# First attention of a decoder stack: weight setup and the keys' maximum as one stage, maxima over 1024 columns at once

## The chip, the cores and the metric

The kernel runs on one core of a Trainium2 chip. The metric is the device time of one execution in microseconds, median of several. All engines of the core (TensorE, VectorE or DVE, ScalarE or ACT, GpSimd or POOL, SyncE or SP) run their own instruction streams and meet at semaphores. The kernel launches once and computes the whole decoder stack.

## The reference, cut to what matters

Two decoder layers over 128 sequences of 64 tokens (8192 tokens, 128 features). The change touches only the first block, an attention with random features:

```python
def _softmax_kernel_feats(data, proj, is_query):
    dn = 1.0 / jnp.sqrt(jnp.sqrt(jnp.float32(data.shape[-1])))
    ratio = 1.0 / jnp.sqrt(jnp.float32(proj.shape[0]))
    data_dash = jnp.einsum('bnhd,md->bnhm', data * dn, proj)
    diag = jnp.sum(jnp.square(data), axis=-1, keepdims=True) * (dn * dn) / 2.0
    if is_query:
        mx = jnp.max(data_dash, axis=-1, keepdims=True)
    else:
        mx = jnp.max(data_dash)
    return ratio * (jnp.exp(data_dash - diag - mx) + EPS_KERN)
...
k = jnp.einsum('bnd,dhk->bnhk', x, Wk)
kf = _softmax_kernel_feats(k, proj, False)
```

For the keys the maximum is taken over everything: all 8192 tokens, 16 heads and 64 features. So the kernel needs one pass over all tokens before the attention itself can begin.

## The kernel before, in words

`program` calls the stages one after the other; each is a `Phase` with its own semaphores, and at its end all engines meet at a barrier. The stages are the weights of the first attention (`setup_l0`), the keys' maximum (`phase_max`), the attention (`phase_performer`), its feed-forward block, and then the stages of the other four blocks, which the change doesn't touch.

**Setup** (`setup_l0`, lines 163 to 239). SP issues 17 loads on one queue (lines 190, 192): Wq, Wk, Wv, Wo, WqT and WkT of 512 KB each, W1 and W2 of 256 KB, eight small ones, and the projection matrix twice at the very end. TensorE and ACT wait for all of them. TensorE then joins projection and weights for queries and for keys (line 205, 16 float32 matmuls of 64 columns each), VectorE scales the results into `Wqp` and `Wkp` (line 214). The five matrices Wq, Wk, Wv, Wqp, Wkp (128x1024) are split into two float16 parts each: ACT writes the high part (line 236), VectorE the low part (line 219).

**Maximum** (`phase_max`, lines 272 to 357). The tokens are taken in 16 groups of 512 columns of the transposed x, two groups to a loop step (U = 2), the first step written out ahead of the loop by `peeled`. For each group SP loads 128x512 (line 301), ACT makes the high part (line 309), POOL the low part (line 317); both parts stay in SBUF (`xT_parts`) for the attention. TensorE then makes 8 tiles of 128x512 in 8 PSUM banks (`dd`), each out of three matmuls by the helper `thrice` (lines 158 to 160). VectorE takes the maximum of each tile (line 346) and folds the 8 columns into `acc` (line 349). TensorE may write a tile again when VectorE has read it (`part_ready`). Behind the loop the 128 maxima are brought to one and sent to all partitions (lines 332, 334, 352 to 356). Then the attention begins, with a barrier and two memsets of POOL (line 463) in front.

The pair of waits that ties TensorE and VectorE:

```python
pe.wait_ge(part_ready, TILES_HM * (U * it + j - 1) + i + 1)
thrice(nc, dd[i][:], [part[:, i, :] for part in Wkp], [part[:, group(it, j)] for part in xT_parts]).then_inc(dd_ready, 1)
...
dve.wait_ge(dd_ready, n)
nc.vector.tensor_reduce(part[j][:, i:i + 1], dd[i][:], AX, ALU.max).then_inc(part_ready, 1)
```

Of the kernel before, what the change touches and what calls it, by code (L numbers as in the profile page):

```python
# [10 lines left out]
ALU = mybir.AluOpType  # L11
# [151 lines left out]
def setup_l0(nc, ph, d, ident):  # L163

    DH, PAIRS = 64, H // 2
    DN = float(DH) ** -0.25
    PROJECTED = ("Wq", "Wk", "Wv", "Wqp", "Wkp")
# [6 lines left out]
    with Phase(nc, "s0") as t:  # L174
        wT = {k: t.sb(k, [P, PAIRS, D]) for k in ("WqT", "WkT")}
        whole = {k: t.sb(k, [P, PAIRS, P]) for k in PROJECTED}
        projT2 = t.sb("projT2", [P, DH])
        b2_rows, low_row = t.sb("b2_rows", [2, D]), t.sb("low_row", [2, 1])
        fused = [t.ps(f"fused{i}", [P, PAIRS, DH]) for i in range(4)]
        loaded, ones_ready, joined, scaled, high_ready, masked = (  # L180
            t.sem(n) for n in ("loaded", "ones_ready", "joined", "scaled", "high_ready", "masked"))
        loads = [(whole["Wq"], d["Wq"]), (whole["Wk"], d["Wk"]), (whole["Wv"], d["Wv"]), (w["Wo"], d["Wo"]), (wT["WqT"], d["WqT"]),
                 (wT["WkT"], d["WkT"]), (w["W1"], d["W1"]), (w["W2"], d["W2"]), (w["b1"], d["b1"]), (b2_rows, d["b2"].to_broadcast([2, D])), (low_row, d["low_row"]),
                 (w["ln1_g"], d["ln1_g"].to_broadcast([P, D])), (w["ln1_b"], d["ln1_b"].to_broadcast([P, D])),
                 (w["ln2_g"], d["ln2_g"].to_broadcast([P, D])), (w["ln2_b"], d["ln2_b"].to_broadcast([P, D]))]
        with nc.Block() as block:
            @block.sync
            def _(sp):
                for dst, src in loads:
                    sp.dma_start(dst[:], src[:]).then_inc(loaded, 16)  # L190
                for half in (slice(0, 64), slice(64, 128)):
                    sp.dma_start(projT2[half, :], d["projT"][:]).then_inc(loaded, 16)

            @block.gpsimd
            def _(pool):
                nc.gpsimd.memset(w["ones2"][:], 1.0).then_inc(ones_ready, 1)

            @block.tensor
            def _(pe):
                pe.wait_ge(loaded, 16 * (len(loads) + 2))  # L200
                for n, name in enumerate(("WqT", "WkT")):
                    for h in range(H):
                        half = slice(64 * (h % 2), 64 * (h % 2) + 64)

                        last = nc.tensor.matmul(fused[2 * n + h % 2][:, h // 2, :], wT[name][half, h // 2, :],
                                                projT2[half, :], start=True, stop=True)
                last.then_inc(joined, 1)

            @block.vector
            def _(dve):  # L210
                dve.wait_ge(joined, 1)
                for n, name in enumerate(("Wqp", "Wkp")):
                    for hh in range(2):
                        last = nc.vector.tensor_scalar(whole[name][:, :, 64 * hh:64 * hh + 64], fused[2 * n + hh][:], DN, None, ALU.mult)
                last.then_inc(scaled, 1)
                for n, k in enumerate(PROJECTED):

                    dve.wait_ge(high_ready, n + 1)
                    nc.vector.scalar_tensor_tensor(w[k][1][:].rearrange("p a b -> p (a b)"), whole[k][:].rearrange("p a b -> p (a b)"), L0_SCALE[k],
                                                   w[k][0][:].rearrange("p a b -> p (a b)"), ALU.mult, ALU.subtract)  # L220
                nc.vector.tensor_scalar(w["less_b1"][:], w["b1"][:], -1.0, None, ALU.mult)
                for n, (rows, parts) in enumerate(((b2_rows, w["b2_parts"]),)):

                    dve.wait_ge(high_ready, len(PROJECTED) + n + 1)
                    nc.vector.tensor_scalar(parts[:], parts[:], low_row[:], None, ALU.mult).then_inc(masked, 1)
                    dve.wait_ge(masked, n + 1)
                    nc.vector.tensor_tensor(parts[:], rows[:], parts[:], ALU.subtract)
                dve.wait_ge(ones_ready, 1)

            @block.scalar  # L230
            def _(act):
                act.wait_ge(loaded, 16 * (len(loads) + 2))
                for n, k in enumerate(PROJECTED):
                    if n == 3:
                        act.wait_ge(scaled, 1)
                    nc.scalar.activation(w[k][0][:], whole[k][:], ACT.Copy, scale=L0_SCALE[k]).then_inc(high_ready, 1)
                for rows, parts in ((b2_rows, w["b2_parts"]),):
                    nc.scalar.activation(parts[:], rows[:], ACT.Copy).then_inc(high_ready, 1)
    return w
# [32 lines left out]
def phase_max(nc, xT, Wkp, shared_mx, xT_parts):  # L272


    GROUP, U, TILES_HM = 512, 2, 8
    steps = TOK // (GROUP * U)
    with Phase(nc, "mx") as ph:
        x_sb = [ph.sb(f"x{j}", [P, GROUP]) for j in range(U)]
        dd = [ph.ps(f"dd{i}", [P, 512]) for i in range(TILES_HM)]
        part = [ph.sb(f"part{j}", [P, TILES_HM]) for j in range(U)]  # L280
        acc = ph.sb("acc", [P, TILES_HM])
# [4 lines left out]
        dd_ready, part_ready, acc_ready, small, moved, high_ready, low_ready = (  # L286
            ph.sem(n) for n in ("dd_ready", "part_ready", "acc_ready", "small", "moved", "high_ready", "low_ready"))
        ident = shared_mx["ident"]
# [3 lines left out]

        with nc.Block() as block:
            @block.sync
            def _(sp):
                def body(it):
                    for j in range(U):
                        if not is_first(it):

                            sp.wait_ge(low_ready, U * it + (j + 1 - U))  # L300
                        sp.dma_start(x_sb[j][:], xT[:, bass.ds((U * it + j) * GROUP, GROUP)]).then_inc(loaded[j], 16)
                peeled(nc.sync, steps, body)

            @block.scalar
            def _(act):
                def body(it):
                    for j in range(U):
                        act.wait_ge(loaded[j], 16 * (it + 1))
                        nc.scalar.activation(xT_parts[0][:, group(it, j)], x_sb[j][:], ACT.Copy).then_inc(high_ready, 1)
                peeled(nc.scalar, steps, body)  # L310

            @block.gpsimd
            def _(pool):
                def body(it):
                    for j in range(U):
                        pool.wait_ge(high_ready, U * it + j + 1)
                        nc.gpsimd.tensor_tensor(xT_parts[1][:, group(it, j)], x_sb[j][:], xT_parts[0][:, group(it, j)], ALU.subtract).then_inc(low_ready, 1)
                peeled(nc.gpsimd, steps, body)

            @block.tensor  # L320
            def _(pe):
                def body(it):
                    for j in range(U):
                        pe.wait_ge(low_ready, U * it + j + 1)
                        for i in range(TILES_HM):
                            if not (is_first(it) and j == 0):

                                pe.wait_ge(part_ready, TILES_HM * (U * it + j - 1) + i + 1)
                            thrice(nc, dd[i][:], [part[:, i, :] for part in Wkp], [part[:, group(it, j)] for part in xT_parts]).then_inc(dd_ready, 1)
                peeled(nc.tensor, steps, body)  # L330
# [6 lines left out]
            def _(dve):  # L337
                nc.vector.memset(acc[:], -3.0e38).then_inc(acc_ready, 1)
                nc.vector.memset(ones_row[:], 1.0)

                def body(it):
                    for j in range(U):
                        for i in range(TILES_HM):
                            n = TILES_HM * (U * it + j) + i + 1
                            dve.wait_ge(dd_ready, n)
                            nc.vector.tensor_reduce(part[j][:, i:i + 1], dd[i][:], AX, ALU.max).then_inc(part_ready, 1)
# [2571 lines left out]
```

## Time and profile before

| what | value |
|---|---|
| median of 3 runs | 4009.61 us (4009.27, 4009.61, 4018.98) |
| the profiled execution, its own time | 4014.4 us |
| its span, first to last instruction | 4012.6 us |
| TensorE busy | 3414.4 us, 85% |
| VectorE busy | 3038.1 us, 76% |
| ScalarE busy | 2356.9 us, 59% |
| GpSimd busy | 1842.3 us, 46% |
| mean granted TensorE clock | 0.915 |

Times in the trace are microseconds from the span's start. A line such as L346 is a line of the kernel; where a helper issues the instruction (lines 158 to 160) the tile's name tells whose it is. `s_` tiles belong to the setup, `mx_` tiles to the maximum, `b_` tiles to the attention. "SPq" is SP's issue of a DMA, "PEld" a weight load of TensorE, and in brackets stands how long an engine sat idle before a row and what ended that.

### The profile page before, as it was taken

The numbers are of one execution on the slowest core, as the hardware profiler recorded it, in microseconds if no ns is written. First come the engines' busy times: TensorE is split into PE (matmuls) and PEld (weight loads), VectorE is DVE, ScalarE is ACT, GpSimd is POOL, SyncE is SP. The second block draws the span as 40 slices with busy tenths as digits, with TensorE's granted clock in tenths as the row PEclk, the third lists the DMA queues.
The fourth block names the chain that finished last, engine by engine and source line by source line (L and its number), as shares of the span: only waits on it lengthen the run. The fifth ranks groups of instructions, "written<-read, shape, count | busy, mean of one in ns | idle before, by whom it ended". The sixth has DMA issues, their size and how long they took to land. (4 is left out here: it accounts for less than half of the span.)

```text
span 4012.6 us, 91730 instructions
## 1 busy us (share of the span) xinstructions
PE 3414.4 (85%) x30917; PEld 2194.5 (55%) x30917; DVE 3038.1 (76%) x6227; ACT 2356.9 (59%) x5257; POOL 1842.3 (46%) x2322
## 2 busy tenths in 40 slices
PE   6899999998665882899999968888399999999998
PEld 3466666665444872566666657777244444444443
DVE  6777777776674662899999948888588888888887
ACT  1355555654763442799899946565355555555555
POOL 1000000000553663677777722222187777778776
PEclk9999999999887775899999978898699999999999
DMA  2000000000112212000000012222376565556663
GB/s 82 6 11 9 10 9 10 10 9 25 43 51 64 67 49 41 17 18 20 18 18 18 12 46 57 55 58 54 110 160 139 128 136 126 131 126 138 132 136 85
DMA packets 279473, 243.93 MB, mean 61 GB/s; under 512 B 57832, under 2 KB 205324, under 8 KB 279308
## 3 DMA queue, kind: packets, MB, share of 16 engines
q1 hardware_dynamic: 267916, 237.21, 24.9%
q10 hardware_dynamic: 11392, 4.79, 0.5%
q8 instruction: 70, 1.15, 0.1%
q14 instruction: 95, 0.78, 0.1%
HBM read 210.34 MB, written 31.59 MB: 60 GB/s over the span
## 5 line engine op out<-in xcount | busy, mean ns | idle before, releaser
L2650 POOL TENSOR_TENSOR d_hidden<-d_gated,d_upper 128x512 f32<-128x512 f32 x528 | 802.2, 1544 | 259.8 <-DVE d_upper L2759 131.7
L2766 DVE TENSOR_TENSOR d_h_low<-d_hidden,d_h_high 128x512 f16<-128x512 f32 x528 | 540.8, 1024 | 118.1 <-ACT d_h_high L2726 116.8
L2720 ACT ACTIVATE d_gated<-d_g 128x512 f32<-128x512 f32 x528 | 315.2, 597 | 493.2 <-PE d_u L2666 493.2
L750 POOL MEMSET f_minus_half<- 128x4 f32 x1 | 0.1, 101 | 864.4 <-POOLq L37 864.4
L2759 DVE TENSOR_TENSOR d_upper<-d_u,d_coef 128x512 f32<-128x512 f32 x512 | 349.2, 682 | 61.4 <-issue 28.2
L2726 ACT ACTIVATE d_h_high<-d_hidden 128x512 f16<-128x512 f32 x528 | 328.4, 622 | 8.2 <-POOL d_hidden L2650 8.2
L1825 ACT ACTIVATE c_sc<-c_sc,c_negmax 128x129 f32<-128x129 f32 x1024 | 326.3, 394 | 9.0 <-issue 4.0
L2664 PE MATMUL d_g<-d_x_high,w_Wg_high 128*128 128x512 f16 x528 | 201.8, 382 | 92.4 <-DVE d_upper L2759 56.1
L1653 POOL TENSOR_TENSOR c_posg<-w_pos,c_gate 128x512 f32<-128x512 f32 x256 | 265.9, 1039 | 0.0
L1732 PE MATMUL c_turned<-all_ident,c_sc 128*128 128x128 f32 x1024 | 180.6, 302 | 35.4 <-ACT c_sc L1825 34.6
L2664 PE MATMUL d_o<-d_h_high,w_Wd_high 128*128 128x512 f16 x528 | 201.4, 381 | 2.0 <-ACT d_h_high L2726 1.6
L2664 PE MATMUL d_u<-d_x_high,w_Wu_high 128*128 128x512 f16 x528 | 202.0, 383 | 0.0
L2665 PE MATMUL d_u<-d_x_high,w_Wu_low 128*128 128x512 f16 x528 | 201.9, 382 | 0.0
L2665 PE MATMUL d_g<-d_x_high,w_Wg_low 128*128 128x512 f16 x528 | 201.8, 382 | 0.0
L2666 PE MATMUL d_u<-d_x_low,w_Wu_high 128*128 128x512 f16 x528 | 201.7, 382 | 0.0
L2666 PE MATMUL d_g<-d_x_low,w_Wg_high 128*128 128x512 f16 x528 | 201.6, 382 | 0.0
L2666 PE MATMUL d_o<-d_h_low,w_Wd_high 128*128 128x512 f16 x528 | 201.4, 381 | 0.0
L2665 PE MATMUL d_o<-d_h_high,w_Wd_low 128*128 128x512 f16 x528 | 201.4, 381 | 0.0
L1937 DVE TENSOR_REDUCE c_negmax<-c_sc 128x4 f32<-128x516 f32 x256 | 176.9, 691 | 8.8
L1935 DVE SCALAR_TENSOR_TENSOR c_sc<-c_scores,c_posg 128x512 f32<-128x512 f32 x256 | 173.4, 678 | 5.3 <-POOL c_posg L1653 2.9
L561 ACT ACTIVATE b_sq<-b_a 128x1024 f32<-128x1024 f32 x64 | 65.6, 1025 | 181.2 <-PE b_a L160 181.2
L1830 ACT ACTIVATE c_pT<-c_turned 128x512 f32<-128x512 f32 x256 | 150.0, 586 | 36.3 <-PE c_turned L1732 36.0
(408 smaller groups left out, 9649.8 us busy)
## 6 DMA issues: line engine op xcount, KB each, us to landing
d_coef<-coefT SPq DMA_DIRECT2D x256, 512.0 KB, 7.2
d_cT<-in_ctxT SPq DMA_DIRECT2D x128, 64.0 KB, 2.0
mx_x<-in_xT SPq DMA_DIRECT2D x16, 256.0 KB
b_x<-in_x SPq DMA_DIRECT2D x64, 64.0 KB
y<-b_y SPq DMA_DIRECT2D x64, 64.0 KB, 1.6
f_y<-y SPq DMA_DIRECT2D x16, 256.0 KB, 3.9
f_x<-in_x SPq DMA_DIRECT2D x16, 256.0 KB, 3.7
x<-f_res SPq DMA_DIRECT2D x16, 256.0 KB, 2.4
```

The source lines that it names most:

```text
L1653: nc.gpsimd.tensor_tensor(posg[a][:], w["pos"][:, hs, :], gate[s][:, hs].unsqueeze(2).to_broadcast([T, 4, T]), ALU.mult).then_inc(posg_rea ...
L1732: last = nc.tensor.transpose(tbank[a % 2][:, i, :], sc[slot(j)][:, 4 * a + i, 0:T], w["ident"][:])
L1825: last = nc.scalar.activation(sc[s][:, h, :], sc[s][:, h, :], ACT.Exp, bias=negmax[s][:, h:h + 1], scale=-1.0)
L1937: nc.vector.tensor_reduce(negmax[s][:, hs], sc[s][:, hs, :], AX, ALU.min).then_inc(top_ready, 1)
L2650: nc.gpsimd.tensor_tensor(hidden[b][:], gated[b][:], upper[b][:], ALU.mult).then_inc(h_ready, 1)
L2664: nc.tensor.matmul(out, weights[0], high, start=start, stop=False)
L2665: nc.tensor.matmul(out, weights[1], high, start=False, stop=False)
L2666: return nc.tensor.matmul(out, weights[0], low, start=False, stop=stop)
L2720: nc.scalar.activation(gated[b][:], ps_g[i][:], ACT.Silu, scale=1.0 / W_SCALE).then_inc(silu_ready, 1)
L2726: nc.scalar.activation(h_high[b][:], hidden[b][:], ACT.Copy).then_inc(h_high_ready, 1)
L2759: nc.vector.tensor_tensor(upper[b][:], ps_u[i][:], coef[c % CBUFS][:, u % CU, :], ALU.mult).then_inc(upper_ready, 1)
L2766: nc.vector.tensor_tensor(h_low[b][:], hidden[b][:], h_high[b][:], ALU.subtract).then_inc(h_low_ready, 1)
```

## The change

`setup_l0` becomes `weights_l0`, which only allocates, and `whole_l0`, which allocates the whole matrices; all work of the setup goes into `phase_max`, so one stage with one barrier stands where there were two.

- SP loads WkT, the projection matrix (twice), group 0 of the tokens, WqT and group 1 first, each with semaphores of their own, and then the other 13 in one row; the loop's token loads come behind them.
- TensorE joins the key weights, then the query weights, into the PSUM tiles `dd[2]` and `dd[3]`, then starts with the products.
- Of the key matrix VectorE scales one half and ACT the other; ACT writes the high part, VectorE the low part. The split of the other four matrices is made behind the last tokens, by ACT (now two instructions for each, a scaling in place and a copy) and POOL (the subtraction, on VectorE before).
- `dd` is 4 tiles of 128x1024 (two banks each) in place of 8 of 128x512. The matmuls are the same 24 for a group; VectorE takes 4 maxima over 1024 columns in place of 8 over 512, and the waits are for a pair of banks.
- The bias rows (three small VectorE instructions) come ahead of the last loop step's maxima.

The diff, cut to its core:

```diff
-        dd = [ph.ps(f"dd{i}", [P, 512]) for i in range(TILES_HM)]
+        dd = [ph.ps(f"dd{i}", [P, 2 * GROUP]) for i in range(WIDE)]
+        fused = dict(Wkp=dd[2], Wqp=dd[3])
...
+                sp.dma_start(whole["WkT"][:], d["WkT"][:]).then_inc(keys_loaded, 16)
+                for half in (slice(0, 64), slice(64, 128)):
+                    sp.dma_start(whole["projT2"][half, :], d["projT"][:]).then_inc(keys_loaded, 16)
+                load_x(0, 0)
+                sp.dma_start(whole["WqT"][:], d["WqT"][:]).then_inc(queries_loaded, 16)
+                load_x(0, 1)
+                for dst, src in rest:
+                    sp.dma_start(dst[:], src[:]).then_inc(rest_loaded, 16)
+                with nc.sync.Fori(1, steps) as it:
                     for j in range(U):
...
+                        sp.wait_ge(low_ready, U * it + (j + 1 - U))
+                        load_x(it, j)
...
+                for j in range(U):
+                    high(0, j)
+                act.wait_ge(joined, 1)
+                out, of = halves("Wkp", 1)
+                nc.scalar.activation(out, of, ACT.Copy, scale=DN).then_inc(other_scaled, 1)
+                act.wait_ge(other_scaled, 1)
+                act.wait_ge(half_scaled, 1)
+                nc.scalar.activation(w["Wkp"][0][:], whole["Wkp"][:], ACT.Copy, scale=L0_SCALE["Wkp"]).then_inc(key_high, 1)
+                act.wait_ge(joined, 2)
+                for hh in range(2):
+                    out, of = halves("Wqp", hh)
+                    nc.scalar.activation(out, of, ACT.Copy, scale=DN).then_inc(query_scaled, 1)
...
+                act.wait_ge(rest_loaded, 16 * len(rest))
+                nc.scalar.activation(w["b2_parts"][:], whole["b2_rows"][:], ACT.Copy).then_inc(row_high, 1)
+                act.wait_ge(query_scaled, 2)
+                for n, k in enumerate(SPLIT):
+                    nc.scalar.activation(whole[k][:], whole[k][:], ACT.Copy, scale=L0_SCALE[k]).then_inc(scaled, 1)
+                    act.wait_ge(scaled, n + 1)
+                    nc.scalar.activation(w[k][0][:], whole[k][:], ACT.Copy).then_inc(split_high, 1)
...
+                for n, k in enumerate(SPLIT):
+                    pool.wait_ge(split_high, n + 1)
+                    nc.gpsimd.tensor_tensor(flat(w[k][1]), flat(whole[k]), flat(w[k][0]), ALU.subtract).then_inc(split_low, 1)
...
+                    for i in range(WIDE):
+                        if not (is_first(it) and j == 0):
+                            pe.wait_ge(part_ready, WIDE * (U * it + j - 1) + i + 1)
+                        elif i == 3:
+                            pe.wait_ge(query_scaled, 2)
+                        for a in range(2):
+                            last = thrice(nc, dd[i][:, GROUP * a:GROUP * (a + 1)], [p[:, 2 * i + a, :] for p in w["Wkp"]], [p[:, group(it, j)] for p in xT_parts])
+                        last.then_inc(dd_ready, 1)
...
+                pe.wait_ge(keys_loaded, 16 * 3)
+                join("WkT", "Wkp")
+                pe.wait_ge(queries_loaded, 16)
+                join("WqT", "Wqp")
+                pe.wait_ge(key_low, 1)
...
+                    for i in range(WIDE):
+                        dve.wait_ge(dd_ready, WIDE * (U * it + j) + i + 1)
+                        nc.vector.tensor_reduce(part[j][:, i:i + 1], dd[i][:], AX, ALU.max).then_inc(part_ready, 1)
```

How the instructions stand. On SP, from the program's start, before:

```order
L190 DMA s_Wq<-in_attn_Wq 128x1024
L190 DMA s_Wk<-in_attn_Wk 128x1024
L190 DMA s_Wv<-in_attn_Wv 128x1024
L190 DMA w_Wo<-in_attn_Wo 128x1024
L190 DMA s_WqT<-in_attn_WqT 128x1024
L190 DMA s_WkT<-in_attn_WkT 128x1024
L190 DMA w_W<-in_attn_W 128x512 x2
```

and with the change:

```order
L263 DMA s_WkT<-in_attn_WkT 128x1024
L265 DMA s_projT<-in_attn_projT 64x64 x2
L261 DMA mx_x<-in_xT 128x512
L267 DMA s_WqT<-in_attn_WqT 128x1024
L261 DMA mx_x<-in_xT 128x512
L270 DMA s_Wq<-in_attn_Wq 128x1024
L270 DMA s_Wk<-in_attn_Wk 128x1024
L270 DMA s_Wv<-in_attn_Wv 128x1024
L270 DMA w_Wo<-in_attn_Wo 128x1024
L270 DMA w_W<-in_attn_W 128x512 x2
```

The key weights moved from place 6 to the front and the projection matrix from the last place to the second; the tokens stood in another stage.

On VectorE, at the same place, before (`s_fused` are the joined weights in PSUM, `mx_part` the maxima of one group):

```order
L214 TENSOR_SCALAR s_Wqp<-s_fused 128x8x64 x2
L214 TENSOR_SCALAR s_Wkp<-s_fused 128x8x64 x2
L219 SCALAR_TENSOR_TENSOR w_Wq_low<-s_Wq,w_Wq_high 128x1024
L219 SCALAR_TENSOR_TENSOR w_Wk_low<-s_Wk,w_Wk_high 128x1024
L219 SCALAR_TENSOR_TENSOR w_Wv_low<-s_Wv,w_Wv_high 128x1024
L219 SCALAR_TENSOR_TENSOR w_Wqp_low<-s_Wqp,w_Wqp_high 128x1024
L219 SCALAR_TENSOR_TENSOR w_Wkp_low<-s_Wkp,w_Wkp_high 128x1024
```

and with the change:

```order
L371 TENSOR_SCALAR s_Wkp<-mx_dd 128x8x64 [waits mx_joined]
L373 SCALAR_TENSOR_TENSOR w_Wkp_low<-s_Wkp,w_Wkp_high 128x1024 [waits mx_key_high]
L362 TENSOR_REDUCE mx_part<-mx_dd 128x1 [waits mx_dd_ready] x4
L365 TENSOR_TENSOR mx_acc<-mx_acc,mx_part 128x4 [waits mx_acc_ready,mx_part_ready]
L362 TENSOR_REDUCE mx_part<-mx_dd 128x1 [waits mx_dd_ready] x4
```

Only one scaling and one subtraction are left ahead of the first maximum; the four other subtractions left this engine. They stand on POOL now, behind its loop over the tokens:

```order
L309 TENSOR_TENSOR parts_xT_low<-mx_x,parts_xT_high 128x512
L314 REGISTER_ALU
L314 COMPARE_AND_BRANCH
L319 TENSOR_TENSOR w_Wq_low<-s_Wq,w_Wq_high 128x1024 [waits mx_split_high]
L319 TENSOR_TENSOR w_Wk_low<-s_Wk,w_Wk_high 128x1024 [waits mx_split_high]
L319 TENSOR_TENSOR w_Wv_low<-s_Wv,w_Wv_high 128x1024 [waits mx_split_high]
L319 TENSOR_TENSOR w_Wqp_low<-s_Wqp,w_Wqp_high 128x1024 [waits mx_split_high]
```

## Rows read from the trace of the kernel before

**Rows 1.** The page, busy time of each engine
```profile
PE 3414.4 (85%) x30917; PEld 2194.5 (55%) x30917; DVE 3038.1 (76%) x6227; ACT 2356.9 (59%) x5257; POOL 1842.3 (46%) x2322
```

**Rows 2.** Timeline, 0 to 60 us: start, duration, engine, line, instruction, count, idle before
```profile
1.98 0.40 SPq L190 DMA_DIRECT2D s_Wq<-in_attn_Wq  x1
...
9.30 1.22 SPq L192 DMA_DIRECT2D s_projT<-in_attn_projT  x2
...
18.40 3.68 PE L205 MATMUL s_fused<-s_projT,s_WqT 64*128 64x64 f32 x32 [18.40 <-DMA s_projT<-in_attn_projT]
...
21.86 3.62 PE L205 MATMUL s_fused<-s_projT,s_WkT 64*128 64x64 f32 x32
25.54 1.29 DVE L214 TENSOR_SCALAR s_Wqp<-s_fused 128x512 f32<-128x512 f32 x2 [25.54 <-PE s_fused L205]
...
29.02 1.04 ACT L236 ACTIVATE w_Wkp_high<-s_Wkp 128x1024 f16<-128x1024 f32 x1
...
32.48 1.22 DVE L219 SCALAR_TENSOR_TENSOR w_Wkp_low<-s_Wkp,w_Wkp_high 128x1024 f16<-128x1024 f32 x1
...
34.94 25.16 SPq L301 DMA_DIRECT2D mx_x<-in_xT  x11
...
37.75 1.26 ACT L309 ACTIVATE parts_xT_high<-mx_x 128x512 f16<-128x512 f32 x2 [7.50 <-DMA mx_x<-in_xT]
38.47 2.26 POOL L317 TENSOR_TENSOR parts_xT_low<-mx_x,parts_xT_high 128x512 f16<-128x512 f32 x2 [36.30 <-ACT parts_xT_high L309]
...
39.68 0.61 PE L158 MATMUL mx_dd<-parts_xT_high,w_Wkp_high 128*128 128x512 f16 x1 [14.19 <-POOL parts_xT_low L317]
```

**Rows 3.** Windows: stretch, its length, busy per engine, granted clock, DMA share, GB/s
```profile
3.00:4.00 1.00, 0.00 (x0) 0.00 (x0) 0.00 (x0) 0.26 (x1) 0.00 (x0) 1.00 0.91 254
...
11.00:12.00 1.00, 0.00 (x0) 0.00 (x0) 0.00 (x0) 0.00 (x0) 0.00 (x0) 1.00 1.01 401
...
16.00:17.00 1.00, 0.00 (x0) 0.00 (x0) 0.00 (x0) 0.00 (x0) 0.00 (x0) 1.00 0.33 36
```

**Rows 4.** Groups, 34 to 130 us: shapes, count, busy us, mean ns, idle before
```profile
L346 DVE TENSOR_REDUCE mx_part<-mx_dd 128x1 f32<-128x512 f32 x128 | 78.5, 680 | 9.8 <-PE mx_dd L160 9.0 <-issue 0.7
L158 PE MATMUL mx_dd<-parts_xT_high,w_Wkp_high 128*128 (+1 forms) x128 | 49.7, 388 | 14.2 <-POOL parts_xT_low L317 14.2
```

**Rows 5.** Timeline, TensorE: clock step at 45 us, last product at 125 us
```profile
45.13 0.38 PE L159 MATMUL mx_dd<-parts_xT_low,w_Wkp_high 128*128 128x512 f16 x1
...
124.99 0.38 PE L160 MATMUL mx_dd<-parts_xT_high,w_Wkp_low 128*128 x1
```

**Rows 6.** Timeline, VectorE: one loop step of two groups, and the end
```profile
97.20 4.87 DVE L346 TENSOR_REDUCE mx_part<-mx_dd 128x1 f32<-128x512 f32 x8 [0.32 <-PE mx_dd L160]
...
107.60 4.87 DVE L346 TENSOR_REDUCE mx_part<-mx_dd 128x1 f32<-128x512 f32 x8 [0.32 <-PE mx_dd L160]
...
123.00 4.87 DVE L346 TENSOR_REDUCE mx_part<-mx_dd 128x1 f32<-128x512 f32 x8
...
128.11 0.16 DVE L352 TENSOR_REDUCE mx_col<-mx_acc 128x1 f32<-128x8 f32 x1
...
129.38 0.16 DVE L356 COPY w_key_max<-mx_dd 128x1 f32<-128x1 f32 x1 [0.47 <-PE mx_dd L334]
```

**Rows 7.** Timeline, GpSimd and VectorE at 48 us
```profile
48.42 1.15 POOL L317 TENSOR_TENSOR parts_xT_low<-mx_x,parts_xT_high 128x512 f32 x1 [2.41 <-ACT parts_xT_high L309]
48.43 1.16 DVE L349 TENSOR_TENSOR mx_acc<-mx_acc,mx_part 128x8 f32<-128x8 f32 x1
```

**Rows 8.** Timeline, VectorE in the attention stage: a 1024-column reduction, then the next
```profile
148.27 1.22 DVE L624 TENSOR_REDUCE b_top<-b_b 128x16 f32<-128x1024 f32 x1 [1.56 <-PE b_b L160]
149.41 0.68 DVE L609 TENSOR_SCALAR b_kf<-b_kf 128x1024 f32<-128x1024 f32 x1
```

**Rows 9.** Windows of a later stage, all f32 on TensorE: columns as in rows 3
```profile
2356.00:2358.00 2.00, 2.00 (x19) 1.96 (x17) 1.52 (x4) 1.01 (x2) 0.00 (x0) 0.50 0.00 0
2358.00:2360.00 2.00, 2.00 (x11) 2.00 (x11) 0.04 (x1) 0.33 (x2) 0.00 (x0) 0.50 0.00 0
```

More of the change, by code:

```diff
@@ L173, in setup_l0 @@
              ln2_g=ph.sb("ln2_g", [P, D]), ln2_b=ph.sb("ln2_b", [P, D]))
[L174 to L238, printed above, removed]
@@ L239, in setup_l0, with whole_l0 @@
-    return w
+    return w
+def whole_l0(t):
+    DH, PAIRS = 64, H // 2
+    whole = {k: t.sb(k, [P, PAIRS, P]) for k in PROJECTED}
+    whole.update({k: t.sb(k, [P, PAIRS, D]) for k in ("WqT", "WkT")})
+    whole.update(projT2=t.sb("projT2", [P, DH]), b2_rows=t.sb("b2_rows", [2, D]), low_row=t.sb("low_row", [2, 1]))
+    return whole
 def setup_cross0(nc, ph, d, ident):
@@ L269, in setup_cross0, with phase_max @@
     return w
[L272 to L275 removed]
+def phase_max(nc, w, whole, d, xT, xT_parts):
+    GROUP, U, PAIRS, WIDE = 512, 2, H // 2, 4
+    DN = 64.0 ** -0.25
+    SPLIT = ("Wq", "Wk", "Wv", "Wqp")
     steps = TOK // (GROUP * U)
@@ L278, in phase_max @@
         x_sb = [ph.sb(f"x{j}", [P, GROUP]) for j in range(U)]
-        dd = [ph.ps(f"dd{i}", [P, 512]) for i in range(TILES_HM)]
-        part = [ph.sb(f"part{j}", [P, TILES_HM]) for j in range(U)]
-        acc = ph.sb("acc", [P, TILES_HM])
+        dd = [ph.ps(f"dd{i}", [P, 2 * GROUP]) for i in range(WIDE)]
+        fused = dict(Wkp=dd[2], Wqp=dd[3])
+        part = [ph.sb(f"part{j}", [P, WIDE]) for j in range(U)]
+        acc = ph.sb("acc", [P, WIDE])
         col = ph.sb("col", [P, 1])
@@ L304, in _, with high @@
             @block.scalar
             def _(act):
-                def body(it):
-                    for j in range(U):
-                        act.wait_ge(loaded[j], 16 * (it + 1))
-                        nc.scalar.activation(xT_parts[0][:, group(it, j)], x_sb[j][:], ACT.Copy).then_inc(high_ready, 1)
-                peeled(nc.scalar, steps, body)
+                def high(it, j):
+                    act.wait_ge(loaded[j], 16 * (it + 1))
+                    nc.scalar.activation(xT_parts[0][:, group(it, j)], x_sb[j][:], ACT.Copy).then_inc(high_ready, 1)
@@ new lines, in _ @@
+                for hh in range(2):
+                    out, of = halves("Wqp", hh)
+                    nc.scalar.activation(out, of, ACT.Copy, scale=DN).then_inc(query_scaled, 1)
+                with nc.scalar.Fori(1, steps) as it:
+                    for j in range(U):
+                        high(it, j)
+                act.wait_ge(rest_loaded, 16 * len(rest))
+                nc.scalar.activation(w["b2_parts"][:], whole["b2_rows"][:], ACT.Copy).then_inc(row_high, 1)
+                act.wait_ge(query_scaled, 2)
@@ L318, in _, with low @@
-                peeled(nc.gpsimd, steps, body)
+                def low(it, j):
+                    pool.wait_ge(high_ready, U * it + j + 1)
+                    nc.gpsimd.tensor_tensor(xT_parts[1][:, group(it, j)], x_sb[j][:], xT_parts[0][:, group(it, j)], ALU.subtract).then_inc(low_ready, 1)
+                nc.gpsimd.memset(w["ones2"][:], 1.0).then_inc(ones_ready, 1)
+                for j in range(U):
+                    low(0, j)
+                with nc.gpsimd.Fori(1, steps) as it:
+                    for j in range(U):
+                        low(it, j)
@@ L320, in _ @@
+                for n, k in enumerate(SPLIT):
+                    pool.wait_ge(split_high, n + 1)
+                    nc.gpsimd.tensor_tensor(flat(w[k][1]), flat(whole[k]), flat(w[k][0]), ALU.subtract).then_inc(split_low, 1)
+                pool.wait_ge(split_low, len(SPLIT))
+                pool.wait_ge(ones_ready, 1)
             @block.tensor
             def _(pe):
-                def body(it):
-                    for j in range(U):
[L324 to L329, printed above, removed]
@@ L330, in _, with join, products @@
-                peeled(nc.tensor, steps, body)
+                def join(source, name):
+                    for h in range(H):
+                        half = slice(64 * (h % 2), 64 * (h % 2) + 64)
+                        last = nc.tensor.matmul(halves(name, h % 2)[1][:, h // 2, :], whole[source][half, h // 2, :], whole["projT2"][half, :], start=True, stop=True)
+                    last.then_inc(joined, 1)
+                def products(it, j):
+                    pe.wait_ge(low_ready, U * it + j + 1)
+                    for i in range(WIDE):
[6 more added lines that the diff above has]
+                        last.then_inc(dd_ready, 1)
@@ L331, in _ @@
+                pe.wait_ge(keys_loaded, 16 * 3)
[3 more added lines that the diff above has]
+                pe.wait_ge(key_low, 1)
+                for j in range(U):
+                    products(0, j)
+                with nc.tensor.Fori(1, steps) as it:
+                    for j in range(U):
+                        products(it, j)
                 pe.wait_ge(small, 1)
@@ L338, in _ @@
                 nc.vector.memset(acc[:], -3.0e38).then_inc(acc_ready, 1)
                 nc.vector.memset(ones_row[:], 1.0)
-                def body(it):
-                    for j in range(U):
[L343 to L346, printed above, removed]
-                        dve.wait_ge(part_ready, TILES_HM * (U * it + j + 1))
-                        dve.wait_ge(acc_ready, U * it + j + 1)
-                        nc.vector.tensor_tensor(acc[:], acc[:], part[j][:], ALU.max).then_inc(acc_ready, 1)
@@ L350, in _ @@
-                peeled(nc.vector, steps, body)
+                dve.wait_ge(joined, 1)
+                out, of = halves("Wkp", 0)
+                nc.vector.tensor_scalar(out, of, DN, None, ALU.mult).then_inc(half_scaled, 1)
+                dve.wait_ge(key_high, 1)
+                nc.vector.scalar_tensor_tensor(flat(w["Wkp"][1]), flat(whole["Wkp"]), L0_SCALE["Wkp"], flat(w["Wkp"][0]), ALU.mult, ALU.subtract).then_inc(key_low, 1)
+                for j in range(U):
+                    tops(0, j)
@@ new lines, in _ @@
+                with nc.vector.Fori(1, steps - 1) as it:
+                    for j in range(U):
+                        tops(it, j)
+                dve.wait_ge(row_high, 1)
+                nc.vector.tensor_scalar(w["less_b1"][:], w["b1"][:], -1.0, None, ALU.mult)
+                nc.vector.tensor_scalar(w["b2_parts"][:], w["b2_parts"][:], whole["low_row"][:], None, ALU.mult).then_inc(row_masked, 1)
+                dve.wait_ge(row_masked, 1)
+                nc.vector.tensor_tensor(w["b2_parts"][:], whole["b2_rows"][:], w["b2_parts"][:], ALU.subtract)
@@ L351, in _ @@
+                for j in range(U):
+                    tops(steps - 1, j)
                 dve.wait_ge(acc_ready, U * steps + 1)
```

44 lines of the change are left out of this document (26 added, 18 removed).

## The prediction

> **What bounds the kernel now.** I read the page first: TensorE is busy 85% of the span [rows 1], but the change touches only its first 130 us, and those must be read by themselves. The timeline from 0 shows three pieces in a row. First nothing computes until all 17 loads have landed: TensorE's first matmul starts at 18.40, released by the projection matrix, the last load issued [rows 2]. Then comes a chain of small steps: joins 18.40 to 25.54, scaling, five splits (the last ends at 32.48 + 1.22 = 33.70), a barrier, the first token load issued at 34.94, its high part at 37.75, its low part, and the first product at 39.68 [rows 2]. From there the products run: the groups list 128 matmuls on each of three lines, 384 in all, and only one idle stretch of TensorE, the 14.2 us ahead of the first [rows 4]. The first 12 start every 0.43 us or so; from 45.13 to 124.99 the other steps are (124.99 - 45.13) / 370 = 0.216 us each [rows 5]. That is 512 columns at 1.2 GHz and then at 2.4 GHz. So TensorE bounds this piece, but VectorE nearly does: one loop step (two groups) takes it 107.60 - 97.20 = 10.40 us with 0.32 idle, against 48 x 0.216 = 10.36 us on TensorE [rows 5, 6], and at the end it is late: the last product ends at 124.99 + 0.38 = 125.37, the final maximum starts at 128.11 [rows 5, 6]. The way from there to the key maximum, 1.4 us, and on to the attention, is the same in both kernels.
>
> **The front.** New start of the products, step by step. SP begins at 1.98 and spends 0.40 on a large issue and 1.22 on the two projection issues [rows 2], so the last load that the key join needs is issued by 3.6. Before, two 256 KB token loads issued from 34.94 were in use at 37.75, 2.8 us later [rows 2]; WkT is as many bytes, and the queue moves 401 GB/s when full [rows 3]. From the second projection issue (3.0) that gives 5.8; I take 5.7, with 5.1 to 6.7 as bounds. The two joins take 25.54 - 18.40 = 7.14 us for both matrices [rows 2], 3.6 each, so keys are joined at 9.3 and queries at 12.8. Between these the key chain runs on VectorE and ACT: half a scaling 0.68 (1.29 for two) on each engine side by side, the high part 1.04, the low part 1.22 [rows 2], about 2.9 with nothing else, so ready at 12.2, under the query join. ACT has first to make the high parts of groups 0 and 1, 0.63 each; group 1 is the fifth load, issued at about 4.7, so in use at 7.5 to 8 and done by 9, just ahead of the key chain. POOL's two low parts (2.26) are done by 10.5. Nothing is later than the query join: **products start at 12.84 in place of 39.68, -26.84 us**. The whole second wait, for tokens, and one barrier are gone in this number.
>
> **The products.** The same 384 matmuls in the same order: 0. Whether the slow 0.43 us steps come again is open: the engine now comes from 7 us of float32 joins instead of 14.2 us of idleness. What rows show is that float32 work need not raise the clock: in a later stage TensorE is busy 2.00 of 2.00 us twice in a row on small float32 matmuls and the granted clock stays 0.50 [rows 9]. So I take 0, bounds 0 and -2.6 (12 x 0.216), and the products end at 12.84 + 85.69 = 98.53. The Trainium skill ("TensorE: Matmul & The Clock Gate", Part 1) says that the slow clock is the default and that sustained matmul activity releases it; by that the joins would do the warming, and the sum would be 2.6 us lower. It comes back as a rival.
>
> **The maxima.** Before, a reduction of 512 costs 4.87 / 8 = 0.61 us in a row [rows 6]. A 1024-column one from two PSUM banks stands in the attention: 1.22 alone, and the next instruction starts 1.14 later [rows 8]. So 8 x 1.14 = 9.1 for a loop step in place of 16 x 0.61 = 9.8, and VectorE's step falls from 10.40 to about 9.75, under TensorE's 10.36. No gain while TensorE bounds, but at the end VectorE is no longer late: it has one 1024 reduction left (1.22) and the fold (0.24 from 127.87 to 128.11), 1.5 us in place of 128.11 - 125.37 = 2.74: **-1.25 us**.
>
> **What moved under cover.** SP's 13 other loads now stand ahead of the loop's token loads. The 17 issues took 8.5 us before [rows 2]; with two token issues the loop's first comes at about 11.5. The bytes (4.0 MB before, 4.5 now) drained by 17 to 18 us before, the end of it slowly, 36 GB/s in small pieces [rows 3]; 0.5 MB more is 1.3 us, and group 2 behind it 0.7. It lands at about 20, and its parts take 0.63 + 1.15: ready at 22. Group 2 is due when groups 0 and 1 are through, 12.84 + 2.6 + 48 x 0.216 = 25.8. Cover of some 4 us; 0. Each later pair comes every 5 us as before, twice as fast as it is used, so the tokens end near 55 us. Behind them ACT's 8 passes of 1.04 and POOL's 4 subtractions, 2.3 each (twice 1.13), end near 66, with 32 us of products left to hide them: 0. The three bias instructions cost VectorE 0.7 us once, inside its new slack.
>
> The moved subtractions can still hurt. At 48.43 VectorE's fold, else 0.17 or so, took 1.16, exactly as long as POOL's subtraction at 48.42 [rows 7]. The Trainium skill ("GPSIMD Engine Reference", 8. Key points) states the cause, a shared SBUF interface and contention when VectorE has two SBUF inputs; rows 7 agree. POOL's new instructions are 2.3 us, so two folds may each wait up to 2.3. TensorE may run three wide tiles ahead, 3.9 us, before it stands. I take 0, bounds 0 and +2.
>
> **Sum.** -26.84 - 1.25 = -28.1 us. Against the profiled execution: 4014.4 - 28.1 = 3986.3. That execution is 4.8 above the median of 4009.6, so against the median **3981.5 us**, 0.7% faster. A measurement of this kernel can tell about 0.3% (12 us) from no change.
>
> **Rivals.**
> - *Warm start* (0.22). The joins lift the clock, all 384 products run at 0.216, the first ones too. For: nothing stands between joins and products now. Against: rows 9. 3978.9.
> - *Backlog or starved supply* (0.14). VectorE falls behind through POOL's long subtractions, or group 2 lands after 25.8, and TensorE stands a few us, perhaps falling back to 1.2 GHz once, which costs 2.6. For: rows 7, and the slow drain in rows 3. Against: 4 us of cover in both. +3 to +6, about 3986.
> - *The order of loads does nothing* (0.07). The loads share the engines, so the first ones land with the last at 18.4. For: all were waited for together before, so no row shows one landing early. The joins would end at 25.54, the key chain is covered, and the products start there: saving 39.68 - 25.54 + 1.25 = 15.4. 3994.2.
> - *Wide maxima bound the stage, slower than before* (0.03). If a reduction across two banks that TensorE is filling in turn is slowed, VectorE bounds. There are 64; VectorE's slack is 0.08 each, and 28.1 / 64 = 0.44, so it decides from 1.14 + 0.52 = 1.66 us each; at 1.8 the stage gains 64 x 0.58 = 37 and the kernel takes 4018. Against: rows 8, where two banks cost the same per column as one.
> - The rest (0.04): the later stages move by themselves, or the start is otherwise late and the result within 0.3%.
>
> **How the numbers follow.** The forecast has 0.50 and gives 3981.5. The range takes in the warm start and the early end of the key load below (3978.9 less 0.6, less 2 for a median that may fall lower), and above the backlog and what the runs of one kernel differ by (three within 10 us, the profiled one 4.8 up): 3976 to 3991. Late loads and slower are left out. Faster by over 0.3% (under 3997.6): 0.94; within 0.3%: 0.03; slower: 0.03.
>
> **What the profile would show.** Right: first join at 5 to 7 us, first product near 12.8 with almost no idle ahead of it, key maximum copied near 101.4 in place of 129.38, wide maxima 1.22 us each with VectorE waiting for TensorE at most of them, one idle stretch of TensorE only. The step from 0.43 to 0.216 some 5 us behind the first product, or none (warm start). Wrong: a first join past 10 us; TensorE idle ahead of the third group; folds of 2 us with TensorE idle behind them; wide maxima over 1.3 us.

## The result and the profile after

The changed kernel takes 3958.76 us (median of 5, 3957.47 to 3965.34) against 4009.27 us for the kernel before (5 runs, 4000.43 to 4018.98): ratio 0.9878, 95% interval 0.9862 to 0.9894. The interval lies wholly below 1: the kernel got faster by 1.2%, and by nearly twice what was forecast: 50.5 us, not 28.1. The profiled execution took 3959.03 us, 55.4 less than the profiled one of before (4014.4, which is itself some 5 above the median); stage by stage I compare these two.

The page of the changed kernel, its span, busy times and one DMA queue; the first two answer to [rows 1]:

```profile
span 3957.2 us, 91525 instructions
...
PE 3417.1 (86%) x30917; PEld 2203.3 (56%) x30917; DVE 3024.6 (76%) x6156; ACT 2363.6 (60%) x5264; POOL 1850.8 (47%) x2326
...
q14 instruction: 68, 0.56, 0.0%
```

The engines are nearly as busy as before (VectorE 13.5 us less, GpSimd 8.5 more, of over 3950). So hardly any work has gone; idle time has. Queue 14, which loads instructions, moved 95 packets before and moves 68 now. I come back to that line.

**The first stage.** The timeline of the first 20 us, which answers to [rows 2]:

```profile
1.97 0.40 SPq L263 DMA_DIRECT2D s_WkT<-in_attn_WkT  x1
...
2.43 1.20 SPq L265 DMA_DIRECT2D s_projT<-in_attn_projT  x2
...
4.78 0.43 SPq L261 DMA_DIRECT2D mx_x<-in_xT  x1
...
6.16 3.67 PE L328 MATMUL mx_dd<-s_projT,s_WkT 64*128 64x64 f32 x32 [6.16 <-DMA s_projT<-in_attn_projT]
...
9.68 3.68 PE L328 MATMUL mx_dd<-s_projT,s_WqT 64*128 64x64 f32 x32
...
9.89 0.69 DVE L371 TENSOR_SCALAR s_Wkp<-mx_dd 128x512 f32<-128x512 f32 x1 [7.63 <-PE mx_dd L328]
...
10.27 0.63 ACT L280 ACTIVATE parts_xT_high<-mx_x 128x512 f16<-128x512 f32 x1 [1.23 <-DMA mx_x<-in_xT]
...
10.81 0.58 ACT L286 ACTIVATE s_Wkp<-mx_dd 128x512 f32<-128x512 f32 x1
...
11.42 1.06 ACT L289 ACTIVATE w_Wkp_high<-s_Wkp 128x1024 f16<-128x1024 f32 x1
...
12.51 1.22 DVE L373 SCALAR_TENSOR_TENSOR w_Wkp_low<-s_Wkp,w_Wkp_high 128x1024 f16<-128x1024 f32 x1 [1.93 <-ACT w_Wkp_high L289]
...
13.79 0.61 PE L158 MATMUL mx_dd<-parts_xT_high,w_Wkp_high 128*128 128x512 f16 x1 [0.43 <-DVE w_Wkp_low L373]
...
16.75 0.61 PE L159 MATMUL mx_dd<-parts_xT_low,w_Wkp_high 128*128 128x512 f16 x1
...
17.17 0.40 PE L160 MATMUL mx_dd<-parts_xT_high,w_Wkp_low 128*128 128x512 f16 x1
```

The last product, TensorE's timeline (answers to [rows 5]):

```profile
98.14 0.38 PE L160 MATMUL mx_dd<-parts_xT_high,w_Wkp_low 128*128 x1
```

VectorE's timeline with two maxima groups of one step, and the end (answers to [rows 6]):

```profile
79.49 4.74 DVE L362 TENSOR_REDUCE mx_part<-mx_dd 128x1 f32<-128x1024 f32 x4 [0.24 <-issue]
84.27 0.16 DVE L365 TENSOR_TENSOR mx_acc<-mx_acc,mx_part 128x4 f32<-128x4 f32 x1
84.37 5.05 DVE L362 TENSOR_REDUCE mx_part<-mx_dd 128x1 f32<-128x1024 f32 x4
...
100.00 0.16 DVE L387 TENSOR_REDUCE mx_col<-mx_acc 128x1 f32<-128x4 f32 x1
...
101.27 0.16 DVE L391 COPY w_key_max<-mx_dd 128x1 f32<-128x1 f32 x1 [0.47 <-PE mx_dd L355]
```

The key maximum is copied at 101.27 in place of 129.38: 28.11 us earlier, the very sum forecast, in part by luck, as the last part tells. The slow steps end at 17.17 after eight matmuls, where twelve were slow before, and the last product ends at 98.14 + 0.38 = 98.52.

**The rest.** Of the 55.4 us between the two profiled executions 27.3 are still without a cause. I looked for the stage in which they lie by the first and last start of one line in each stage. At the attention's first maximum the distance is 28.0 us (135.3 to 107.3), at the start of the last stage, the mixture of experts, 25.6; so between them nothing was won, 2.4 were lost. Then the last stage itself, ACT's gate of which there are 528 (duration min, median and max in ns, then first and last start), before:

```profile
L2720 ACT ACTIVATE d_gated<-d_g x528: 597/597/599, 2896.7 to 3997.3; 128x512 f32<-128x512 f32 x176
```

and with the change:

```profile
L2755 ACT ACTIVATE d_gated<-d_g x528: 597/597/599, 2871.1 to 3941.8; 128x512 f32<-128x512 f32 x176
```

3997.3 - 2896.7 = 1100.6 us before, 3941.8 - 2871.1 = 1070.7 now: **29.9 us in a stage whose code the change doesn't touch**. With the 25.6 ahead of it that makes 55.5, the whole difference. The waits inside its loop (in total, times, longest), before:

```profile
PE d_g L2664 <- DVE d_upper L2759: 43.2, 25, 4.3
...
DVE d_upper L2759 <- issue: 28.2, 5, 5.9
```

after:

```profile
PE d_g L2699 <- DVE d_upper L2794: 23.5, 20, 1.4
...
DVE d_upper L2794 <- PE d_u L2701: 3.6, 10, 0.4
```

Five times VectorE sat idle, for 5.6 us in the mean, before its first instruction of a loop step, and nothing in the profile released it ("issue"). Five is the number of times that this loop jumps back: the stage has eight steps, the first and the last are written out, and the loop between them runs six rounds. With the change the five are gone. One of them in VectorE's timeline, before:

```profile
3162.22 0.68 DVE L2766 TENSOR_TENSOR d_h_low<-d_hidden,d_h_high 128x512 f16<-128x512 f32 x1
3168.80 0.69 DVE L2759 TENSOR_TENSOR d_upper<-d_u,d_coef 128x512 f32<-128x512 f32 x1 [5.91 <-issue]
```

and the windows around it (PE, PEld, DVE, ACT, POOL busy, granted clock, DMA share, GB/s):

```profile
3160.00:3164.00 4.00, 4.00 (x20) 1.85 (x19) 2.86 (x3) 2.24 (x5) 2.72 (x2) 1.00 0.67 200
3164.00:3168.00 4.00, 1.33 (x7) 0.39 (x4) 0.00 (x0) 1.11 (x2) 0.03 (x1) 1.00 0.46 122
3168.00:3172.00 4.00, 2.36 (x6) 0.87 (x7) 2.96 (x4) 0.00 (x0) 2.28 (x2) 0.53 0.01 2
```

VectorE ends a step at 3162.90 and begins the next at 3168.80. TensorE runs dry behind it (busy 1.33 of 4 us), and the granted clock falls to half for some of the time that follows. What VectorE waited for shows in the DMA view, in the line of queue 14. From 3160 to 3170, around this one stretch, before:

```profile
q14 instruction: 3, 0.02, 0.8%
```

Over the loop, before (3140 to 3870):

```profile
q14 instruction: 26, 0.21, 0.1%
```

and after (3100 to 3840):

```profile
q14 instruction: 3, 0.02, 0.0%
```

26 packets of instructions (8 KB each, 0.21 MB by 26) against 3, and these 3 come when the loop is through: from 3100 to 3810 queue 14 has no packet at all with the change. So before, code was loaded again at every jump back of the loop. That it is VectorE's code is an inference up to here; e1 and e2 below test it.

### The profile page after: what moved, and what is told of

The parts are those of the page before. It is cut to its first block and busy times, and to the rows that moved or that the text cites. A ratio compares the mean times of both kernels' runs of the same rounds, so it can differ in the third digit from the quotient of the medians.

```text
span 3957.2 us, 91525 instructions
## 1 busy us (share of the span) xinstructions
PE 3417.1 (86%) x30917; PEld 2203.3 (56%) x30917; DVE 3024.6 (76%) x6156; ACT 2363.6 (60%) x5264; POOL 1850.8 (47%) x2326
## 5 line engine op out<-in xcount | busy, mean ns | idle before, releaser
L2198 POOL TENSOR_TENSOR d_kB<-d_kT,w_variant 128x512 f32<-128x512 f32 x64 | 73.2, 1144 | 211.7 <-ACT d_kT L2352 211.7
```

## The experiments

**Is it the place of VectorE's instructions?** The change took 23 instructions out of VectorE's stream ahead of the last loop (2325 stand there in place of 2348; counted in the program, without branches and without the waits that are instructions of their own). TensorE lost 10, ACT gained 5. With branches and waits 3043 instructions stand there in place of 3068, which is 25 fewer, so the 23 below bring the loop back to within two instructions of its old place. To tell the engines apart I gave only VectorE its 23 back, as memsets while it is idle:

```diff
+        filler = ph.sb("filler", [P, 128])
...
                 nc.vector.memset(ones_row[:], 1.0)
+                for n in range(23):
+                    nc.vector.memset(filler[:, n:n + 1], 0.0)
```

> The changed kernel with 23 tiny memsets more on VectorE at its start, where it sits idle from 2.3 to 9.9 us, so that its last loop stands at the same place of VectorE's instruction stream as before (2348 instructions ahead of it; 2325 with the change). Theory 1, the 27 us beyond the first stage come from code loading on VectorE in the last stage's loop: the five idle stretches of some 5.6 us that end in 'issue' come back there, the last stage takes 1100 us again in place of 1070, total 3980 to 3990. Theory 2, TensorE's code or its clock history does it: nothing changes, 3959. Theory 3, it is only scatter between executions: no steady difference, within 4 us of the changed kernel. The first stage ends at 101.3 in all three.

Measured: 3989.08 us (4 runs, 3986.17 to 3991.16), ratio to before 0.9935 (0.9918 to 0.9951); key maximum at 102.29. VectorE's group in the last stage:

```profile
L2797 DVE TENSOR_TENSOR d_upper<-d_u,d_coef 128x512 f32<-128x512 f32 x512 | 349.1, 682 | 64.1 <-issue 30.7 <-PE d_u L2704 11.2 <-DMA d_coef<-coefT 10.8
```

The five "issue" stretches are back, 30.7 us, and queue 14 shows 94 packets. The 23 memsets take 0.58 us together at the program's start and cost 30 us more than 3.1 ms later. TensorE's stream was the changed one; its code is not the cause, nor is scatter. (The key maximum came 1.0 us later than expected: the products began at 14.17, and eleven of them were slow.)

The other way round, the kernel before with 105 memsets ahead of `dve.wait_ge(joined, 1)`:

> The kernel before with 105 tiny memsets on VectorE ahead of its first wait, hidden behind the loads; 105 = 128 - 23, so if code is loaded in blocks of 128 instructions (8 KB at 64 bytes) the last loop stands in its block as in the changed kernel. Theory 1 with that block: the five stretches go, total about 4009 - 25 = 3984, with the first stage ending at 129.4 as before. Theory 1 with another block size: no change. Theories 2 and 3: no change, 4009.

Measured: 3989.64 us (3978.51 to 3995.48) against 4014.70, ratio 0.9929 (0.9908 to 0.9949); the first stage still ends at 127.92. VectorE's group:

```profile
L2762 DVE TENSOR_TENSOR d_upper<-d_u,d_coef 128x512 f32<-128x512 f32 x512 | 349.1, 682 | 30.5 <-DMA d_coef<-coefT 11.1 <-PE d_u L2669 6.5 <-issue 0.4
```

0.4 us of "issue" in place of 28.2, 70 packets on queue 14. So the kernel before could have had these 25 us by itself (by the interval, 20 to 37; this kernel's four runs lie 17 us apart). A control with 41 memsets in the same spot:

> A control for e2: the kernel before with 41 memsets in place of 105, so that 2389 instructions stand ahead of VectorE's last loop, a place that had the five stretches in e6. By the border theory nothing changes against before, ratio 1.000, and the stretches are there. If the memsets in the kernel before gain by themselves (by timing, not by place), it is faster, 4000 or less.

Measured: 4011.29 us against 4014.98, ratio 0.9989 (0.9975 to 1.0003), "issue" 30.9 us, 94 packets. Memsets alone do nothing; the place does.

**Where are the good places?** Three more in the changed kernel:

> The changed kernel with 12 tiny memsets more on VectorE at its start: 2337 instructions ahead of its last loop, between the changed kernel (2325, no stretch) and e1 (2348, five stretches of some 6 us). If a border of a code block decides, it is one or the other and nothing between: last stage 1070 or 1100 us, total 3959 or 3988. If the stretch grew with each instruction it would be about half, 3974.

Measured: 3954.69 us, ratio to before 0.9855 (0.9833 to 0.9877), no stretch.

> The same with 64 memsets more (2389 instructions ahead of the last loop), 41 behind e1, 41 ahead of the place that is the changed kernel's again if code comes in blocks of 128. Theory with a border: either clean, 3959, or five stretches, 3988; it tells on which side the clean places lie. A theory in which the number of instructions matters, not the place, has stretches at 23 and so also at 64.

Measured: 3988.43 us, 0.9934 (0.9909 to 0.9960), five stretches of 5.2 to 5.4 us.

> The changed kernel with 90 memsets more (2415 ahead of the last loop), between e6 (2389, stretches) and the place of e2 (2453, none). Either clean, 3959, or five stretches, 3988; it narrows down the share of places that are clean, which is the chance that an unrelated edit to VectorE's stream costs or gains some 28 us.

Measured: 3962.70 us, 0.9856 (0.9827 to 0.9885), no stretch, 69 packets on queue 14. (The page of e6 has 95 there, that of e5 68.)

| instructions ahead of VectorE's last loop | kernels | last stage, us | "issue" stretches |
|---|---|---|---|
| 2325, 2326 (e4) | after, e7, e4 | 1070.7 (after), 1070.9 (e7), 1069.3 (e4) | none |
| 2329 | e8 | 1069.4 | none |
| 2337 | e5 | 1069.0 | none |
| 2348 | before, e1 | 1100.6, 1101.6 | five |
| 2357 | e3 | 1098.7 | five |
| 2389 | e6, e9 | 1095.8, 1095.9 | five |
| 2415 | e10 | 1069.1 | none |
| 2453 | e2 | 1071.0 | none |

All or nothing, with borders between 2337 and 2348 and between 2389 and 2415, and the place of 2325 good again 128 further on. A sum that grows with the number of instructions is out. With branches and waits counted, the kernels made from the one before (before, e2, e9) stand two instructions further than the table says, so e2 is 130 and not 128 behind the changed kernel; the order of the rows stays, and both borders with it.

**The terms of the first stage.** Narrow maxima in the new stage (eight PSUM tiles of 512 columns, `WIDE = 8`, one `thrice` to a tile):

```diff
-                        for a in range(2):
-                            last = thrice(nc, dd[i][:, GROUP * a:GROUP * (a + 1)], [p[:, 2 * i + a, :] for p in w["Wkp"]], [p[:, group(it, j)] for p in xT_parts])
+                        last = thrice(nc, dd[i][:], [p[:, i, :] for p in w["Wkp"]], [p[:, group(it, j)] for p in xT_parts])
```

> The changed kernel with 8 PSUM tiles of 512 columns and 8 maxima a group, as before; all else kept. By my sum the key maximum comes 1.25 us later (101.27 to 102.5), since VectorE is late at the end again; a rival says that the wide maxima also keep TensorE from standing still, and then the products themselves end later than 98.5. VectorE has 32 instructions more ahead of its last loop than with the change, 9 more than before; by theory 1 the last stage may lose its 28 us again for that alone, total 3960 to 3990.

Measured: 3994.29 us, 0.9956 (0.9940 to 0.9973), with the stretches; 4 us above the range expected. The key maximum comes 0.96 us later, not 1.25, though the products began 0.6 earlier. The stage's end, VectorE and TensorE:

```profile
100.66 0.16 DVE L386 TENSOR_REDUCE mx_col<-mx_acc 128x1 f32<-128x8 f32 x1
...
102.23 0.16 DVE L390 COPY w_key_max<-mx_dd 128x1 f32<-128x1 f32 x1 [0.67 <-PE mx_dd L354]
```

```profile
96.97 0.38 PE L160 MATMUL mx_dd<-parts_xT_high,w_Wkp_low 128*128 x1
100.87 0.37 PE L352 MATMUL mx_dd<-all_ident,mx_col 128*1 128x128 f32 x1 [3.52 <-DVE mx_col L386]
```

TensorE's last product ends 96.97 + 0.38 = 97.35 (the products started at 13.19 and only some five of them were slow), and VectorE takes until 100.66 to begin the final maximum, 3.3 us late; in the changed kernel it is 1.5. TensorE has no wait for VectorE in the loop either way, so within this stage the wide maxima bring what stands behind the last product, 1.8 us here, and nothing else.

The load order of before in the new stage (Wq, Wk, Wv, Wo, WqT, WkT and the rest, the projection last, then groups 0 and 1):

> The changed kernel with the loads issued in the order of before (keys sixth, projection last, then two token groups), still one stage. My sum of the front: the joins start at 18.4, end at 25.5, the tokens are there at about 20, so the products start at 25.8 and the key maximum comes 12 us later than in the changed kernel, 113.3; total 3971. VectorE's instructions stand where they do with the change, so no stretch in the last loop. If the front's gain came from dropping the barrier and the second wait alone, the key maximum stays near 101 to 105.

Measured: 3971.48 us, 0.9899 (0.9877 to 0.9921); key maximum at 113.57. TensorE's timeline:

```profile
19.06 3.68 PE L330 MATMUL mx_dd<-s_projT,s_WkT 64*128 64x64 f32 x32 [19.06 <-DMA s_projT<-in_attn_projT]
...
26.08 0.61 PE L158 MATMUL mx_dd<-parts_xT_high,w_Wkp_high 128*128 128x512 f16 x1
```

The order of the loads is worth 12.3 us (113.57 - 101.27); what is left of the 28.1, some 16, came from making one stage out of two, and the tail (1.3).

The four late subtractions on VectorE, ahead of the last loop step's maxima:

```diff
+                for n, k in enumerate(SPLIT):
+                    dve.wait_ge(split_high, n + 1)
+                    nc.vector.tensor_tensor(flat(w[k][1]), flat(whole[k]), flat(w[k][0]), ALU.subtract).then_inc(split_low, 1)
```

> The changed kernel with the four late subtractions on VectorE instead of GpSimd, ahead of the last loop step's maxima, where VectorE has little slack. By my sum of the cover: 4 x 1.2 = 4.9 us more on VectorE, TensorE may run 3.9 us ahead, so it stands about 1 us or more, and the key maximum comes 2 to 5 us later, 103 to 106; total 3961 to 3964. A rival says that GpSimd's long subtractions cost VectorE as much where they are now: then nothing changes.

Measured: 3966.29 us, 0.9878 (0.9848 to 0.9907), too scattered (3952.95 to 3971.05) for a verdict by the total; the stage itself is clear, key maximum at 106.07, 4.8 us late. The first of VectorE's subtractions, the wait of TensorE, and a window just behind it (columns as in [rows 3]):

```profile
90.56 1.21 DVE L383 TENSOR_TENSOR w_Wq_low<-s_Wq,w_Wq_high 128x1024 f16<-128x1024 f32 x1
```

```profile
PE mx_dd L158 <- DVE mx_part L359: 2.7, 1, 2.7
```

```profile
96.00:98.00 2.00, 1.55 (x4) 0.65 (x5) 2.00 (x3) 0.00 (x0) 0.00 (x0) 0.53 0.00 0
```

TensorE stood 2.7 us, and when it went on the granted clock was 0.53 from 96 to 98. So the pause was paid for twice: of the 4.8 us, 0.3 are a later start of the products (14.12), 2.7 the pause, and the remaining 1.8, by my estimate, the slow matmuls behind it. On GpSimd the same four cost the stage nothing.

**The clock.** Nine float16 matmuls on a tile of ones ahead of the key join:

```diff
+                pe.wait_ge(warm_ready, 1)
+                for _ in range(9):
+                    nc.tensor.matmul(dd[0][:, 0:512], warm[:, 0:128], warm[:], start=True, stop=True)
                 pe.wait_ge(keys_loaded, 16 * 3)
```

> The changed kernel with nine float16 matmuls of 512 columns on a tile of ones ahead of the key join, while the loads are under way. If the clock rises before the joins and float32 joins hold it, the products start at 0.216 us a step: the 8 slow steps go, key maximum 1.7 us earlier, at 99.6. If the joins let it fall, the products start slowly again and nothing is gained. If the joins themselves run faster at the higher clock, they take less than 3.5 us each.

Measured: 3961.05 us, 0.9873 (0.9855 to 0.9892), not to be told from the changed kernel. TensorE:

```profile
2.69 3.90 PE L345 MATMUL mx_dd<-mx_warm 128*128 128x512 f16 x9 [2.69 <-DVE mx_warm L371]
6.52 2.00 PE L329 MATMUL mx_dd<-s_projT,s_WkT 64*128 64x64 f32 x32
9.21 3.23 PE L329 MATMUL mx_dd<-s_projT,s_WqT 64*128 64x64 f32 x32 [0.69 <-DMA s_WqT<-in_attn_WqT]
13.32 0.61 PE L158 MATMUL mx_dd<-parts_xT_high,w_Wkp_high 128*128 128x512 f16 x1 [0.88 <-DVE w_Wkp_low L378]
...
16.28 0.53 PE L159 MATMUL mx_dd<-parts_xT_low,w_Wkp_high 128*128 128x512 f16 x1
16.64 0.38 PE L160 MATMUL mx_dd<-parts_xT_high,w_Wkp_low 128*128 128x512 f16 x1
```

and two windows, with the granted clock third from the end:

```profile
8.00:9.00 1.00, 0.52 (x10) 0.38 (x8) 0.43 (x1) 0.58 (x1) 0.34 (x1) 1.00 1.10 338
10.00:11.00 1.00, 1.00 (x14) 1.00 (x12) 0.00 (x0) 0.97 (x3) 0.49 (x1) 0.50 1.05 410
```

The key join takes 2.00 us in place of 3.67, and then the clock falls: 0.50 granted between 10 and 11, in the middle of the query join, while TensorE is busy all the time. Ahead of that join it had stood 0.69 us, waiting for WqT. The products start slowly again, at 13.32, with eight slow ones. So one join ran at the high clock, but the clock did not last through the second; whether the float32 work or the pause of 0.69 us let it fall, this run does not tell apart. In the changed kernel, where no such pause stands between the joins, 7 us of them didn't raise it.

## Why the prediction was wrong

The sum of the first stage came out right, in part by luck, and what the prediction missed lay in another stage. Point by point:

- *The front.* Products from 13.79 in place of the forecast 12.84. The key load was in use at 6.16 (forecast 5.7). The rest comes from group 1's high part, which I had put at 9 at the latest: its load, issued behind WqT's on the same queue, landed late, so that it ran only at 10.27 and held ACT's half of the key scaling to 10.81, while VectorE had made its half at 9.89. So the key chain ended last (12.51 + 1.22 = 13.73), not the query join (13.36). -25.89 in place of -26.84.
- *The products.* 98.52 - 13.79 = 84.73 us in place of 85.69, since eight were slow and not twelve. The warm start did not come: the rows on float32 work [rows 9] were the better guide. The rule of the Trainium skill ("TensorE: Matmul & The Clock Gate", Part 1), that sustained matmul activity releases the slow clock, holds for the float16 products here but not for 7 us of these joins. What sets the number of slow steps isn't settled: it was 12 (before), 8 (after), 8 (e4), 11 (e1) and 5 (e3).
- *The maxima.* 100.00 - 98.52 = 1.48 in place of 2.74: -1.26 against -1.25. e3 gives 1.8 for it by another way.
- *Under cover.* Hidden, all of it: TensorE has no wait in the loop. GpSimd's new subtractions take 2.14 each and end at 64.7 (forecast 66). The harm that I had feared from them did come, once: a fold of VectorE that began during the last one took 1.18 us in place of 0.16 and ended with it. Its cost of 1.0 us stayed inside VectorE's slack:

```profile
56.29 2.14 POOL L319 TENSOR_TENSOR w_Wq_low<-s_Wq,w_Wq_high 128x1024 f16<-128x1024 f32 x1 [0.97 <-ACT w_Wq_high L303]
...
62.58 2.13 POOL L319 TENSOR_TENSOR w_Wqp_low<-s_Wqp,w_Wqp_high 128x1024 f16<-128x1024 f32 x1
...
63.55 1.18 DVE L365 TENSOR_TENSOR mx_acc<-mx_acc,mx_part 128x4 f32<-128x4 f32 x1
```

  e8 measured what the cover is worth, 4.8 us.
- *The sum of the stage* was -28.1, and -28.11 was measured. That it fits to 0.01 us is luck: two errors, 0.95 us (the products began late) and 0.96 us (fewer of them were slow), cancelled.
- **The step that failed is a silent one: the sum puts all that stands behind the key maximum at 0, without a reason.** "The later stages move by themselves" stood only among the rest, at 0.04 and with no price. In its place the runs showed the last stage shorter by 29.9 us (2.4 were lost on the way to it), because VectorE's stream ahead of its loop was 23 instructions shorter, 25 with branches and waits, and the code was no longer loaded again at the loop's five jumps back. The signs were in the profile of before: 28.2 us of "issue" in front of one line of VectorE, in five stretches of 5.4 to 5.9 us; the fifth part of its page says "issue 28.2". The 2.4 us lost between the stages stay without a cause. Apart from [rows 9] I read no row behind 175 us. e1 and e2 carry the cause: giving VectorE alone its 23 instructions back costs the 30 us again, and shifting the old kernel wins 25.
- Not tried: which block, kept or dropped, makes the border. The period of 128 instructions rests on one pair (2325 and 2453). The Trainium skill ("Runtime: NRT & Kernel Launch", Instruction fetch mechanics) describes such a cause: a taken branch whose target isn't in the engine's instruction window forces a fetch before execution goes on. The traces agree: all five stretches stand behind a jump back to the loop's start. That section gives the refill unit as 16 KB of 256 instructions. The packets that these runs drop or gain, on queue 14, are of 8 KB, and the measurement decides. By the 64 bytes an instruction that its figures imply, 8 KB would be 128 instructions, an estimate; the clean places agree with it, but do not prove it.

## What to carry to other kernels

When an edit adds or removes instructions ahead of a long loop, look in the old profile for idle stretches that end in "issue" once per loop step, and at the packets of the instruction queue; each such loop is worth its stretch times its jumps back, in either direction, whatever the edit is meant for. To price an edit, compare stage by stage, and test a surprise in an untouched stage with a few fillers on one engine at a time. The edit proper went nearly as the rows said: load first what the first instruction needs, and let the rest land behind work that is bound by another engine.

## What the hardware showed that I had not expected

- 23 memsets at the start moved the end by 30 us. In all kernels that have the five stretches, each is 5.2 to 6.3 us long, always of VectorE, and TensorE's clock was granted at 0.53 over the 4 us behind one of them. The same loop is free of them at 2337 instructions and has all five at 2348.
- The granted clock fell to 0.50 while TensorE was 100% busy with float32 matmuls of 64 columns (e4, 10 to 11 us), 0.8 us and more after a pause of 0.69 us; the key join takes 2.00 us at the high clock and 3.67 at the low.
- Two-bank maxima took 1.20 to 1.23 us each while TensorE filled other banks, what the attention's reduction had shown [rows 8]; four in a row took 4.60 us when VectorE was late.
